# The carry of a selective scan: a strided DMA on SyncE in place of a GpSimd copy

## The reference, cut to what matters

```
xz = x @ in_proj.T;  x, z = split(xz)               # 1024 channels each
x = silu(causal_conv4(x) + conv_b)
dt, B, C = split(x @ x_proj.T)                      # 64, 16, 16
dt = softplus(dt @ dt_proj.T + b)
h_t = exp(dt_t * A) * h_{t-1} + dt_t * B_t * x_t    # for 1024 channels x 16 states
y_t = sum_n h_t[n] * C_t[n] + D * x_t
out = (y * silu(z)) @ out_proj.T
x1 = layernorm(hidden + out)
result = layernorm(x1 + ffn(x1))                    # ffn: two matmuls, weights in {-1, 0, 1}
```

## Time and profile before

| | |
|---|---|
| median of three runs | 5414.19 us (5403.51 to 5415.39) |
| profiled execution, its own time | 5411.71 us |
| its span | 5409.9 us |
| mean granted TensorE clock | 0.927 of full speed |
| busy: PE, DVE, ACT, POOL | 4586.6, 4053.4, 3570.6, 3170.8 us |
| DMA engines, mean busy share in the mixer's phase | 0.30 |

### The profile page before, as it was taken

One profiled execution on the slowest core, in us unless ns is written; L12 is line 12 of the kernel. 1 busy time (PEld: TensorE's weight loads), 2 busy tenths in 40 slices (PEclk: granted clock), 3 DMA queues, 4 the chain that ended last, 5 costly groups with the idle time before them and its releaser, 6 DMA issues. The chain is left out here.

```text
span 5409.9 us, 85208 instructions
## 1 busy us (share of the span) xinstructions
PE 4586.6 (85%) x23362; PEld 3179.0 (59%) x23362; DVE 4053.4 (75%) x4775; ACT 3570.6 (66%) x6726; POOL 3170.8 (59%) x2474
## 2 busy tenths in 40 slices
PE   5979788888989788889897988888787588888888
PEld 3656555555656565556565655556564477777776
DVE  5888888888889798988888888888886534444444
ACT  5878787878788778788887878787885122222222
POOL 4786868687878778787868686868785000000000
PEclk8999999999989899999898989999998799999999
DMA  2322333233333323232223332332232200000000
GB/s 93 96 89 90 99 92 100 88 102 98 98 103 90 99 89 101 88 101 94 96 90 97 93 96 91 103 97 98 87 93 68 79 31 31 31 31 31 31 31 16
DMA packets 233278, 436.73 MB, mean 81 GB/s; under 512 B 23872, under 2 KB 24000, under 8 KB 232320
## 3 DMA queue, kind: packets, MB, share of 16 engines
q1 hardware_dynamic: 232832, 431.55, 25.3%
HBM read 397.38 MB, written 34.08 MB: 80 GB/s over the span
## 5 line engine op out<-in xcount | busy, mean ns | idle before, releaser
L696 DVE TENSOR_TENSOR_SCAN h<-decay,carry,dbu 128x512 f32<-128x512 f32 x2048 | 2529.3, 1270 | 306.4 <-ACT decay L488 139.1
L445 POOL TENSOR_TENSOR dbu<-dtx,bb 128x1024 f32<-128x1024 f32 x1024 | 2461.5, 2404 | 5.5 <-issue 2.3
L488 ACT ACTIVATE decay<-dt,aneg 128x512 f32<-128x512 f32 x2048 | 1431.6, 701 | 698.5 <-DVE h L696 693.8
L871 PE MATMUL ht<-ident,h 128*128 128x128 f32 x8192 | 1338.9, 291 | 603.9 <-DVE h L696 451.6
L871 PEld LDWEIGHTS ht<-ident,h 128*128 128x128 f32 x8192 | 1011.5, 149 | 1329.3 <-issue 801.7
L502 ACT ACTIVATE ch<-ht,ct 128x256 f32<-128x256 f32 x3328 | 1404.2, 482 | 86.7 <-PE ht L871 85.0
L821 PE MATMUL gemm<-xt,win 128*128 128x512 f32 x2048 | 1074.4, 610 | 10.8 <-DMA win<-w_in 7.1
L876 PEld LDWEIGHTS y<-ident,ch 128*128 128x128 f32 x6656 | 790.2, 143 | 406.9 <-issue 363.1
L876 PE MATMUL y<-ident,ch 128*128 128x128 f32 x6656 | 892.2, 278 | 4.2 <-ACT ch L502 1.9
L419 POOL TENSOR_TENSOR carry<-h,ones_pair 128x2 f32<-128x2 f32 x1022 | 272.0, 266 | 862.9 <-DVE h L696 852.6
L1104 ACT ACTIVATE hr<-hidden_ps,b1c 128x512 f32<-128x512 f32 x256 | 174.3, 687 | 773.6 <-PE hidden_ps L1215 773.6
(11 more groups left out here) (90 smaller groups left out, 3588.5 us busy)
## 6 DMA issues: line engine op xcount, KB each, us to landing
bb<-b_rows SPq DMA_DIRECT2D x1024, 256.0 KB, 3.3
win<-w_in SPq DMA_DIRECT2D x256, 256.0 KB, 3.6
xt<-x_cm SPq DMA_DIRECT2D x16, 1024.0 KB, 6.6
xres<-x_tm SPq DMA_DIRECT2D x16, 1024.0 KB, 6.8
x<-xres SPq DMA_DIRECT2D x16, 1024.0 KB, 5.2
xr<-x SPq DMA_DIRECT2D x16, 1024.0 KB, 5.3
out<-xr SPq DMA_DIRECT2D x16, 1024.0 KB, 4.3
raw<-w SPq DMA_DIRECT2D x2, 4096.0 KB, 17.8
```

What stands on the lines that cost most here:

```text
L445: nc.gpsimd.tensor_tensor(dbu[:, u % 2, :, :], dtx[:, pair(q), :], bb[:, u % BB_RING:u % BB_RING + 1, :].to_broadcast([P, 2, TC]), ALU.mul ...
L488: nc.scalar.activation(DA[j][:, :], dt[:, c.par, i, :], ACT.Exp, scale=aneg[:, i, n:n + 1])\
L696: nc.vector.tensor_tensor_scan(h[:, H_SLOT[u], j, :], DA[j][:, :], dbu[:, u % 2, j, :], carry[:, c.par, n, i:i + 1], ALU.mult, ALU.add).th ...
L871: ins = nc.tensor.transpose(HT[k][:, tb % 2, j * P:(j + 1) * P], h[:, H_SLOT[u], j, tb * P:(tb + 1) * P], ident[:, :])
```

## The change: what it does

`save_state` moves from POOL's list to SP's. It becomes a DMA from `h` to `carry`, from SBUF to SBUF. The last dimension of the source has the stride of a whole row, so each number is an element of its own: 128 x 2 x 1 elements of 4 bytes. It stands five units behind (`SAVE_LAG`), after the load of `bb` of the unit; the last five units of a chunk are saved in the next chunk's list. The semaphore `carried` becomes three, one for each slot of `h`, and DVE's wait names the slot's own one. The copies on POOL are gone, and nothing else changes on it.

```diff
+SAVE_LAG = 5
+SAVES = [16 * H_SLOT.count(r) for r in range(3)]
 ...
-        carried = sem("carried")
+        carried = [sem(f"carried{r}") for r in range(3)]
 ...
+            def save_state(c, u):                                   # on SP
+                q, n, r = u // NS, u % NS, H_SLOT[u]
+                wait(sp, scanned, c, SCANS, 2 * u + 2)
+                sp.dma_start(carry[:, c.par, n, pair(q)].rearrange("p (j o) -> p j o", o=1), h[:, r, :, TC - 1:TC],
+                             allow_slow_non_contiguous=True).then_inc(carried[r], 16)
 ...
                     load_bb(c, u)
+                    if u >= SAVE_LAG:
+                        save_state(c, u - SAVE_LAG)
+                    elif not is_first:
+                        save_state(p, UNITS - SAVE_LAG + u)
 ...
+            for u in range(UNITS - SAVE_LAG, UNITS):
+                save_state(last, u)
 ...
-            def save_state(c, u):                                   # on POOL
-                q, n = u // NS, u % NS
-                wait(pool, scanned, c, SCANS, 2 * u + 2)
-                nc.gpsimd.tensor_tensor(carry[:, c.par, n, pair(q)], h[:, H_SLOT[u], :, TC - 1], ones[:, :], ALU.mult)\
-                    .then_inc(carried, 1)
 ...
-                    if u >= 2:
-                        save_state(c, u - 2)
-                    elif not is_first:
-                        save_state(p, UNITS - 2 + u)
 ...
-                    wait(dve, carried, c.near(back), UNITS, user + 1)
+                    r = H_SLOT[u]
+                    wait(dve, carried[r], c.near(back), SAVES[r], 16 * (H_SLOT[:user].count(r) + 1))
```

More of the change, by code:

```diff
@@ L83, in h_user_before @@
     return -1, max(v for v in range(UNITS) if H_SLOT[v] == H_SLOT[u])
-COUNTS = sorted({1, 4, 8, 16, 64, 128, 256, 2 * len(BY_ACT), len(BY_ACT), TB * len(BY_DVE), NB * (KC - 1)})
+SAVES = [16 * H_SLOT.count(r) for r in range(3)]
+COUNTS = sorted({*SAVES, 1, 4, 8, 16, 64, 128, 256, 2 * len(BY_ACT), len(BY_ACT), TB * len(BY_DVE), NB * (KC - 1)})
 KINDS = {"x": NB, "z": NB, "xd": 1, "ct": 1, "dt": NB, "o": TB}
```

## The result

The changed kernel takes 5477.14 us, the median of four runs (5471.49 to 5486.48), against 5412.06 us for the kernel before (four runs). The ratio is 1.0116, 95% interval 1.0098 to 1.0135. It is slower by some 65 us. The forecast was 5401 us with a range of 5382 to 5454 us, so the time lies outside the range, and the sign of the forecast was wrong.

What follows compares the result with a forecast made beforehand. DVE's scans carry the mixer's order, with POOL's late products ending 132.8 us of idle time. From 5411.71 us, -20 for POOL and +8 for landing waits gave 5400, with half of 2.5 us given back 5401 us; range 5382 to 5454 us.

Steps and rivals of the forecast that it cites:

- POOL's gain: Mixer phase: without the copy, 170 late products on POOL each start 0.14 to 0.27 us sooner; 20 us gained.
- the 63.5 us put down to the copy: DVE's idle time before scans in 97 waits recorded as ended by POOL's copy; the prediction assigned it to POOL's product.
- The row of DVE's waits for POOL: Expected sign: the two rows of DVE waiting for POOL become one, of 100 to 120 us.
- The landing: The save DMA issued by SP lands 2.9 us after issue, with 2.0 to 6 us as bounds.
- The wait at unit 1: At chunk starts DVE waits 0.9 us for unit 63's save, about 16 times; 0.5 us each charged, 8 us.
- the dense stretch: Units 40 to 43: 5.5 us until the slot's next use against 3.1 us for the save; hidden, no cost.
- `win`: Weight load queued on SP behind a save: issued 0.45 us later with 0.95 us to spare; nothing charged.
- unit 60: Two units after unit 58: the save lands 0.7 us before the scan of this unit starts; hidden.
- The slow landing: Rival, chance 0.18: the save takes 5 us or more to land, DVE waits at unit 1 and unit 60; 5454 us.
- a landing of 6 us: Within the slow landing rival: dense stretches join the waits, costing 138 us, time 5550 us.
- What is removed: Part on POOL's 1022 copies, 272.0 us busy: gain is only one step of 0.14 to 0.27 us at 170 late products.
- ACT takes the gain back: ACT's decay stands right behind POOL before scans, so three quarters of the 27 us gain were taken, 20 us.

Runs made afterwards that it cites:

- small products at 62 units: Changed kernel plus a 128x2 product of ones on POOL ahead of the product dbu of units 2 to 63: 5398.35 us, ratio 0.9973.
- where the collision is out: dt<-dt,soft moved one unit behind rounded<-soft, in the kernel before (5395.61 us, ratio 0.9959) and in the changed kernel (5376.89 us, ratio 0.9936).
- taking the waits away: Changed kernel with dt<-dt,soft one unit later and, on SP, each save ahead of the bb load: 5385.24 us, ratio 0.9943.
- three small products: Changed kernel plus a 128x2 product of ones on POOL ahead of the product dbu of units 7, 9 and 54 alone: 5377.05 us, ratio 0.9934.
- `DT_SUM_AT` on the kernel before: Kernel before with only dt<-soft,dt of the third and fourth channel pair moved from units 12 and 13 to 13 and 14: 5396.21 us, ratio 0.9968.
- half products: Changed kernel plus half of the product dbu (128x512) on POOL ahead of the full one at units 7, 9 and 54: 5416.59 us, ratio 1.0005.
- the parted pair: Changed kernel with dt<-dt,soft on DVE one unit later, no longer right behind rounded<-soft: 5376.89 us, ratio 0.9936.

## Why the prediction was wrong, point by point

- *POOL's gain.* Predicted 20 us. Measured 21 us between small products at 62 units and at 3 units, and 12 to 19 us net for the whole change where the collision is out. That the sizes agree is partly luck. The 20 us were to come as idle time before late scans; most of what came was shorter operations of DVE (14.4 of the span's 21.5 us in the one pair, 18.6 of 20.8 in the other), which the prediction doesn't have. Whether the 63.5 us put down to the copy were the product's can't be read from their going, since they would go with the copy in either case. The row of DVE's waits for POOL was to be 100 to 120 us and came to 75.6.
- *The landing.* Predicted 2.9 us, and measured 2.8. The reason was half wrong: with no load just ahead of it the transfer lands in 1.8 us, and it is the `bb` load ahead of it that makes it 2.8. The chunk start shows that order, SP after:

```profile
1378.92 0.32 SPq L285 DMA_DIRECT2D bb<-b_rows  x1
1379.40 0.61 SPq L291 DMA_DIRECT2D carry<-h  x1
```

  The issue with its register work costs 0.73 us, from the save to the `win` behind it, and not the 0.45 us that I took:

```profile
1210.41 0.60 SPq L291 DMA_DIRECT2D carry<-h  x1
1211.14 0.53 SPq L279 DMA_DIRECT2D win<-w_in  x1
```

  `win` comes later by that much, but it landed in 2.9 us in the median where it took 3.6 before, and PE's only wait for it is the 7.1 us of before.
- *The wait at unit 1.* Predicted about 16 waits of 0.9 us; there were 13 at unit 1 and one of 1.0 us at unit 60 of the first chunk, 12.0 us in all. The term of 8 us in the time was too high: taking the waits away gave nothing. That the dense stretch and `win` would cost nothing was right, and so it was for unit 60 in the 15 other chunks.
- *The rivals.* The slow landing would have put the time at 5454 us and looks nearest by number. It is wrong in substance, since DVE waited 12.0 us for landings and not 16 x (3.0 + 1.4) = 70. Its figure for a landing of 6 us is added up wrongly: by its own steps 3.5 + 2.4 = 5.9 us stand where it has 4.9, which makes 154 us and not 138. Nothing hangs on it.
- *The step that failed* is the sentence under "What is removed", "What a product gains is the distance from the copy's start to its own", with all that follows from it: I charged the copy's removal only at waits on semaphores. The copy did a second thing, it stood between a product of 2.36 us and an operation of DVE that can't run beside it. Its removal cost 90.3 us on 64 instances of `dt<-dt,soft`, a term that the prediction put at nothing. No rival named this, so the range did not hold it either. The trace of before had shown it: copies up to 1192 ns, products of 3.3 us, `dt<-dt,soft` at 1.2 or at 3.5 us. The page's mean for the copy, 266 ns against 190 in the common case, was the hint, and I passed over it.
- *ACT takes the gain back.* Predicted as a quarter. Waits for the decay rose by 62.1 us as those for POOL fell by 57.2. That was named as a sign of being wrong, but they rose as much in the runs that were faster than before (199.5 us with three small products), so these sums say who was last and not what the time does.

What stays open: the 17 us of `DT_SUM_AT` on the kernel before, and 15.2 us in 6 cases that POOL waited for its own issue in the changed kernel (2.3 us in 8 before). Five of the six, 2.8 to 3.7 us each, stand before the first product of a loop iteration, as here:

```profile
1374.24 4.65 POOL L450 TENSOR_TENSOR dbu<-dtx,bb 128x1024 f32<-128x1024 f32 x2 [2.80 <-issue]
```

Such pauses of over 2 us are in the changed kernel and in the four made from it that put nothing ahead of the products (7.0 to 21.9 us in all), and in none of the kernels with small or half products or with copies on POOL. DVE's waits for POOL before unit 0 are 34.0 us in the changed kernel, 20.3 before, and 11.0 with three small products. So they are a cost of the changed kernel, some 14 us of waiting at that place, and their cause is not shown. They are not what made it slow: the parted pair has them too (9.0 us) and is 100 us faster.

## What to carry to other kernels

When an instruction is taken off GpSimd, look at what stood on VectorE around it, not only at who waits for it. In these traces the two engines were served in the order in which their operations came, so a short operation between two long ones could be what let the other engine in. Such time shows as a longer operation and not as idle: compare minimum, median and maximum of each operation before reading waits, and put VectorE's operations that GpSimd holds where GpSimd is waiting for VectorE anyway. What it gives back depends on the place: taking a held operation out gave 100 us at units 5, 7 and 52, and 7 of 29.6 us at units 12 and 13, where GpSimd was behind in any case.

## What the runs showed of the hardware that was not expected

- A 128x1024 operation of VectorE on two SBUF tensors took 1.21 us alone, and 2.30 or 3.38 us when a GpSimd product of 512 or 1024 columns had come first. A GpSimd product of 2.36 us took 3.2 to 3.4 us when VectorE's had.
- Of two VectorE operations back to back, the second did not keep its turn: a GpSimd instruction that was waiting under the first went in between, in 3 of 4 places of each chunk (units 5, 7 and 52; 3.38 us there, 1.21 us at unit 50).
- The first of the two, with one SBUF input, was held as well: 0.67 us at least and up to 2.25 us.
- A scan with one operand in PSUM took 1268 to 1270 ns on average in every run, and never more than 1287 ns, whatever GpSimd did.
- A DMA of 256 elements of 4 bytes inside SBUF landed in 1.8 us, less than any other transfer of these traces in its median; right behind a 256 KB load on the same queue it took 2.8 us. Its issue took 0.60 us against 0.32 us.
